# One written-out order of stages for a fused expert and attention block, with the maxima rows on Sync's queue

## The reference

```
# block 0, per sequence
nx = layer_norm(x) * gamma + beta
w  = softmax((nx @ Wq) @ (ctx @ Wk).T / sqrt(128));  evidence = w @ (ctx @ Wv)
c  = concat(nx, evidence, cond)
p  = softmax(c @ router_W + router_b)                      # 3 experts
h  = silu(c @ e_w1 + e_b1);  routed = sum_e p_e * (h_e @ e_w2_e + e_b2_e)
x  = x + sigmoid(silu(c @ gate_w1 + b) @ gate_w2 + b) * (routed @ out_w + out_b)
# block 1
m  = silu(cond) @ ada_w + ada_b                            # 6 shifts, scales, gates
x  = x + gate_msa * (attention16(qkv(norm(x) * (1 + scale) + shift)) @ self_o + b)
x  = x + attention16(q = norm(x) @ q_w, k, v = ctx @ kv_w) @ cross_o + b
x  = x + gate_mlp * (gelu((norm(x) * (1 + scale) + shift) @ w1 + b) @ w2 + b)
```

## Time and profile before

| | us |
|---|---|
| median of 3 runs | 326.23 |
| lowest, highest | 324.36, 326.57 |
| the profiled execution, its own time | 325.7 |
| its span | 323.9 |
| mean TensorE clock granted in it | 0.91 |

### The profile page before, as it was taken

The page is one execution under the profiler, slowest core; times in us unless marked ns, Lnnn a source line. Parts: engine busy times, 40 slices in busy tenths (PEclk is TensorE's granted clock), DMA queues, the critical chain, the costliest instruction groups (busy, mean ns, idle before and its releaser), DMA issues.

```text
span 323.9 us, 4780 instructions
## 1 busy us (share of the span) xinstructions
PE 255.5 (79%) x1784; PEld 145.0 (45%) x1802; DVE 180.1 (56%) x390; ACT 147.5 (46%) x271; POOL 43.8 (14%) x54
## 2 busy tenths in 40 slices
PE   3779999799467889279989899887997766748676
PEld 2765657358012344134534444543643433436356
DVE  6643317658979758337889757983131533250331
ACT  1213241542005476236665577569386342724442
POOL 1200420806001072000100010020010012000120
PEclk9999999999758999969999999999899795776979
DMA  7999900037410015620030002000003000200000
GB/s 205 393 131 173 169 2 0 0 98 177 134 55 5 3 51 148 133 63 2 2 92 9 6 3 87 14 5 0 18 17 84 2 3 2 78 20 21 0 0 32
DMA packets 15456, 19.71 MB, mean 61 GB/s; under 512 B 3234, under 2 KB 13474, under 8 KB 14442
## 3 DMA queue, kind: packets, MB, share of 16 engines
q1 hardware_dynamic: 15014, 19.22, 23.8%
q10 hardware_dynamic: 420, 0.20, 0.2%
HBM read 16.19 MB, written 3.03 MB: 59 GB/s over the span
## 4 chain that ended last, share of the span: by engine, by line
PE 54%; DVE 25%; ACT 7%; DMA 7%; issue 5%; SPq 1%; POOL 0%; ACTq 0%; DVEq 0%; POOLq 0%
PE ps L1172 47%; DVE neg_max L1050 7%; DMA Qs<-max_rows 4%; DVE normed L863 4%; DVE neg_max L1059 3%; ACT region L766 3%; PE ps L1430 2%; PE ps L1200 2%; DVE routed L1007 1%; DVE stats L847 1%; DMA Qs<-q_scr 1%; DMA x_sb<-in_x 1%; ACT max_rows L752 1%; PE ps L1375 1%; DVE mean_var L850 1%
## 5 line engine op out<-in xcount | busy, mean ns | idle before, releaser
L766 ACT ACTIVATE region<-ps 128x512 f32<-128x512 f32 (+1 forms) x160 | 86.7, 595 | 51.7 <-PE ps L1172 51.2
L1050 DVE TENSOR_REDUCE neg_max<-ps 128x2 f32<-128x1024 f32 x64 | 77.4, 1222 | 27.1 <-PE ps L1172 26.1
L1172 PE MATMUL ps<-Qs,k_room 128*128 128x256 bf16 x256 | 42.3, 283 | 10.8 <-DMA Qs<-max_rows 7.2
L1172 PE MATMUL ps<-k_room,Qs 128*128 128x512 bf16 x111 | 38.7, 426 | 7.5 <-DVE neg_max L1050 4.9
L1172 PE MATMUL ps<-region,V 128*32 128x256 f32 x512 | 41.3, 401 | 0.8 <-DMA Qs<-q_scr 0.5
L582 POOL TENSOR_TENSOR rstd<-var_eps,minus_half 128x2 f32<-128x2 f32 (+1 forms) x12 | 9.7, 811 | 218.0 <-DVE var_eps L852 218.0
L1172 PEld LDWEIGHTS ps<-Qs,k_room 128*128 128x128 bf16 x256 | 22.3, 100 | 30.4 <-ACT region L766 15.9
L1172 PEld LDWEIGHTS ps<-region,V 128*32 128x32 f32 x512 | 10.6, 109 | 22.7 <-issue 20.2
L1059 DVE TENSOR_REDUCE neg_max<-ps 128x8 f32<-128x616 f32 x16 | 12.0, 792 | 13.4 <-PE ps L1172 13.3
L1172 PEld LDWEIGHTS ps<-k_room,Qs 128*128 128x128 bf16 x128 | 11.7, 102 | 17.0 <-DVE neg_max L1050 13.1
L752 ACT ACTIVATE max_rows<-ps 24x256 bf16<-24x256 bf16 (+1 forms) x12 | 4.5, 374 | 31.1 <-PE ps L1375 31.1
(11 more groups left out here) (159 smaller groups left out, 344.7 us busy)
## 6 DMA issues: line engine op xcount, KB each, us to landing
Qs<-q_scr SPq DMA_DIRECT2D x24, 192.0 KB
k_room<-k_scr SPq DMA_DIRECT2D x4, 576.0 KB
...
q_scr<-q_parts SPq DMA_DIRECT2D x8, 192.0 KB, 2.0
...
w_attn<-in_w_attn SPq DMA_DIRECT2D x1, 896.0 KB, 10.5
...
```

The lines of the kernel that those rows point to most:

```text
L766: nc.scalar.activation(probs[0:rows_, s % UNITS, j0:j0 + CT // 2, :], ps[0:rows_, EXP0 + e % 2, :].rearrange("p (j n) -> p j n", n=TU), AC ...
L1050: nc.vector.tensor_reduce(neg_max[:, b, t, h:h + MH], ps[:, bank:bank + MH, :], axis=AX, op=ALU.max, negate=True).then_inc(max_read, 1)
L1172: return nc.tensor.matmul(out, lhsT, rhs, start=start, stop=stop)
```

## The change

`plan()` goes, and a text `ORDER` takes its place, word by word a stage. The table has more kinds of stage than before, as steps that hung on another stage now have a place of their own: `rows` (the DMA of maxima rows, issued by Sync and no longer by ScalarE), `send_keys`, `send_queries`, `load_keys`, `load_queries`, `load_cross`, `expert_bias`, `fold`, `add_bias`, `context_parts` and `weights:3`.

- Group self.0.0 is split, transposed and sent in two halves of four heads; exps of its first halves come first for all four key tiles.
- The products for the context leave `weights:2` for `weights:3`, behind queries:0, in banks MAX0 and MAX0 + 1; ScalarE copies them out and GpSimd splits the keys. `weights:2` moves ahead of hidden:0.4.
- route_norm:1 and expert_bias:1 come after the queries of sequence 1.
- Sequence 2's norm, keys, queries and values are placed singly among maxima and exps.
- `add_bias` waits for the normalisation behind its residual (`normed_ready`).
- `load_exp:1` is gone; mlp_down:0, project:self.3 and others stand elsewhere.

```diff
+ORDER = """
+scores:0 bias:0 scores_norm:0 scores_T:0 scores:1 evidence:0 bias:1 route:0 scores_norm:1 route_norm:0 hidden:0.0
+scores_T:1 hidden:0.1 hidden:0.2 hidden:0.3 weights:0 weights:1 weights:2 fold:0 expert_bias:0 hidden:0.4 hidden:0.5
+expert:0.0 hidden:0.6 evidence:1 gate:0 expert:0.1 expert:0.2 fold:1 route:1 expert:0.3 gated:0 stats:1.0 hidden:1.0
+hidden:1.1 apply:1.0 hidden:1.2 hidden:1.3 norm_T:1.0 add_bias:self.1 keys:0 queries:0 add_bias:self.0 weights:3
+send_keys:0 send_queries:0 load_keys:0.0 route_norm:1 load_queries:0 load_keys:0.1 load_queries:1 hidden:1.4
+hidden:1.5 values:0 hidden:1.6 expert_bias:1 gate:1 expert:1.0 expert:1.1 expert:1.2 context_parts:0 expert:1.3
+gated:1 max:0 max:1 max:2 max:3 max_split:self.0.0.0 max:4 max_T:self.0.0.0 max:5 max:6 max:7 rows:self.0.0.0 max:8
+max_split:self.0.0.1 max:9 max:10 max_T:self.0.0.1 load_exp:0 max:11 stats:1.1 rows:self.0.0.1 max:12 apply:1.1
+max:13 exp:self.0.0.0.0 exp:self.0.0.1.0 max:14 add_bias:self.2 max:15 max_split:self.0.1 norm_T:1.1 max:16
+exp:self.0.0.2.0 weigh:self.0.0.0.0 max_T:self.0.1 max:17 exp:self.0.0.3.0 weigh:self.0.0.1.0 rows:self.0.1 keys:1
+exp:self.0.0.0.1 max:18 weigh:self.0.0.2.0 max:19 weigh:self.0.0.3.0 queries:1 add_bias:self.3 weigh:self.0.0.0.1
+max:20 send_keys:1 exp:self.0.0.1.1 send_queries:1 exp:self.0.0.2.1 load_keys:1.0 load_queries:2 exp:self.0.0.3.1
+load_keys:1.1 exp:self.0.1.0.0 max:21 weigh:self.0.0.1.1 exp:self.0.1.0.1 max:22 exp:self.0.1.1.0 weigh:self.0.0.2.1
+max:23 load_queries:3 weigh:self.0.0.3.1 max_split:self.1.0 max_T:self.1.0 keep:self.0.0 weigh:self.0.1.0.0
+rows:self.1.0 max:24 max:25 exp:self.0.1.1.1 weigh:self.0.1.0.1 max:26 exp:self.0.1.2.0 exp:self.0.1.2.1
+weigh:self.0.1.1.0 values:1 weigh:self.0.1.1.1 exp:self.0.1.3.0 values_T:self.0.0 max:27 weigh:self.0.1.2.0
+exp:self.0.1.3.1 weigh:self.0.1.2.1 max:28 exp:self.1.0.0.0 max:29 weigh:self.0.1.3.0 exp:self.1.0.0.1 max:30 max:31
+exp:self.1.0.1.0 weigh:self.0.1.3.1 max_split:self.1.1 keep:self.0.1 exp:self.1.0.1.1 weigh:self.1.0.0.0
+max_T:self.1.1 exp:self.1.0.2.0 max:32 values_T:self.0.1 weigh:self.1.0.0.1 exp:self.1.0.2.1 max:33 heads_T:self.0
+weigh:self.1.0.1.0 max:34 exp:self.1.0.3.0 rows:self.1.1 weigh:self.1.0.1.1 project:self.0 stats:2.0
+exp:self.1.0.3.1 max:35 apply:2.0 max:36 weigh:self.1.0.2.0 exp:self.1.1.0.0 weigh:self.1.0.2.1 exp:self.1.1.0.1
+norm_T:2.0 max:37 add_bias:cross.0 weigh:self.1.0.3.0 query:0 max:38 exp:self.1.1.1.0 exp:self.1.1.1.1 max:39
+load_cross:0 weigh:self.1.0.3.1 keep:self.1.0 max_split:self.2.0 exp:self.1.1.2.0 max:40 max_T:self.2.0
+rows:self.2.0 max:41 weigh:self.1.1.0.0 max:42 weigh:self.1.1.0.1 exp:self.1.1.2.1 max:43 weigh:self.1.1.1.0
+exp:self.1.1.3.0 weigh:self.1.1.1.1 values_T:self.1.0 exp:self.1.1.3.1 max:44 weigh:self.1.1.2.0 exp:self.2.0.0.0
+cross_max:0.0 cross_max:0.1 cross_max:0.2 exp:self.2.0.0.1 max:45 cross_max:0.3 max_split:cross.0.0 exp:self.2.0.1.0
+weigh:self.1.1.2.1 weigh:self.1.1.3.0 max:46 max:47 exp:self.2.0.1.1 max_T:cross.0.0 max_split:self.2.1
...
+weigh:self.2.1.2.0 exp:self.3.0.1.0 max:60 weigh:self.2.1.2.1 apply:3.0 max:61 exp:self.3.0.1.1 norm_T:3.0
+exp:self.3.0.2.0 max:62 max:63 max_split:self.3.1 weigh:self.2.1.3.0 add_bias:mlp.0 weigh:self.2.1.3.1 mlp_up:0.0
+keep:self.2.1 mlp_up:0.1 max_T:self.3.1 weigh:self.3.0.0.0 exp:self.3.0.2.1 values_T:self.2.1 weigh:self.3.0.0.1
+rows:self.3.1 weigh:self.3.0.1.0 heads_T:self.2 exp:self.3.0.3.0 project:self.2 exp:self.3.0.3.1 exp:cross.1.0.0.0
+weigh:self.3.0.1.1 weigh:self.3.0.2.0 stats:2.2 apply:2.2 add_bias:cross.2 exp:cross.1.0.0.1 weigh:self.3.0.2.1
+norm_T:2.2 exp:cross.1.1.0.0 weigh:self.3.0.3.0 query:2 load_cross:2 exp:cross.1.1.0.1 weigh:self.3.0.3.1
+keep:self.3.0 exp:self.3.1.0.0 exp:self.3.1.0.1 weigh:cross.1.0.0.0 values_T:self.3.0 weigh:cross.1.0.0.1 mlp_down:0
+keep:cross.1.0 exp:self.3.1.1.0 weigh:cross.1.1.0.0 values_T:cross.1.0 exp:self.3.1.1.1 weigh:cross.1.1.0.1
+keep:cross.1.1 exp:self.3.1.2.0 weigh:self.3.1.0.0 values_T:cross.1.1 cross_max:2.0 weigh:self.3.1.0.1 cross_max:2.1
+exp:self.3.1.2.1 cross_max:2.2 cross_max:2.3 exp:self.3.1.3.0 heads_T:cross.1 weigh:self.3.1.1.0 exp:self.3.1.3.1
+max_split:cross.2.0 max_T:cross.2.0 project:cross.1 rows:cross.2.0 weigh:self.3.1.1.1 weigh:self.3.1.2.0 stats:3.1
+weigh:self.3.1.2.1 weigh:self.3.1.3.0 weigh:self.3.1.3.1 keep:self.3.1 values_T:self.3.1 apply:3.1 heads_T:self.3
+exp:cross.2.0.0.0 project:self.3 add_bias:mlp.1 stats:2.3 exp:cross.2.0.0.1 norm_T:3.1 weigh:cross.2.0.0.0 apply:2.3
+add_bias:cross.3 norm_T:2.3 weigh:cross.2.0.0.1 keep:cross.2.0 query:3 load_cross:3 values_T:cross.2.0
+exp:cross.2.1.0.0 weigh:cross.2.1.0.0 exp:cross.2.1.0.1 weigh:cross.2.1.0.1 keep:cross.2.1 mlp_up:1.0 mlp_up:1.1
+cross_max:3.0 cross_max:3.1 cross_max:3.2 cross_max:3.3 max_split:cross.3.0 values_T:cross.2.1 max_T:cross.3.0
+rows:cross.3.0 mlp_down:1 heads_T:cross.2 exp:cross.3.0.0.0 project:cross.2 exp:cross.3.0.0.1 weigh:cross.3.0.0.0
+stats:3.2 weigh:cross.3.0.0.1 exp:cross.3.1.0.0 keep:cross.3.0 exp:cross.3.1.0.1 values_T:cross.3.0
+weigh:cross.3.1.0.0 weigh:cross.3.1.0.1 keep:cross.3.1 apply:3.2 norm_T:3.2 values_T:cross.3.1 heads_T:cross.3
+project:cross.3 add_bias:mlp.2 mlp_up:2.0 stats:3.3 mlp_up:2.1 apply:3.3 norm_T:3.3 add_bias:mlp.3 mlp_up:3.0
+mlp_up:3.1 mlp_down:2 mlp_down:3
+"""
...
-        DELAY = dict(values_T=1, heads_T=2, project=3, stats=3, apply=5, norm_T=6, query=7, cross_max=13, rows=4,
-                     mlp_up=7, mlp_down=10)
-        NEXT = (0, 2, 3, 5, 7, 8)
...
+        CONTEXT_BANK = (MAX0, MAX0 + 1)
...
+            def load_cross(u):
+
+                sp.wait_ge(exp_raw, group_scored(("self", u, NG - 1)))
                 sp.wait_ge(q_out, 16 * Q_WRITES[("query", u)])
                 q_rows(u, NU + u)
...
+            def move_maxima(*group):
+
+                n = split_turn(*group)
+                u = group[1]
+                h0, nh = split_heads(*group)
+                sp.wait_ge(mT_ready, n + 1)
+                sp.dma_start(Qs[u][MROW:MROW + NPART, h0:h0 + nh, :],
+                             max_rows[0:NPART * nh, n % 2, :]).then_inc(m_in[n % 2], 16)
...
+            def split_context_keys():
+
+                pool.wait_ge(kc_ready, 1)
+                own(nc.gpsimd.tensor_copy(kc_parts[:, 0, :, :], kcf[:, :, :]))
+                own(nc.gpsimd.tensor_tensor(kc_rest[:, :, :], kcf[:, :, :], kc_parts[:, 0, :, :], ALU.subtract))
+                own(nc.gpsimd.tensor_copy(kc_parts[:, 1, :, :], kc_rest[:, :, :]))
+                tell(nc.gpsimd.tensor_tensor(kc_parts[:, 2, :, :], kc_rest[:, :, :], kc_parts[:, 1, :, :],
+                                             ALU.subtract), kc_split, 1)
...
                 if kind == "self":
-                    pool.wait_ge(x1_ready, b + 1)
+                    pool.wait_ge(normed_ready, NORM_TURN[(1, b)] + 1)
...
+            def keep_context():
+                act.wait_ge(ones_set, B)
+                act.wait_ge(kc_raw, 1)
+                nc.scalar.activation(kcf[:, :, 0:L], ps[:, CONTEXT_BANK[0], 0:B * L].rearrange("p (b n) -> p b n", b=B),
+                                     ACT.Identity, bias=col("kv_k")).then_inc(kc_ready, 1)
...
-                act.wait_ge(mT_ready, n + 1)
-                act.dma_start(Qs[u][MROW:MROW + NPART, h0:h0 + nh, :],
-                              max_rows[0:NPART * nh, n % 2, :]).then_inc(m_in[n % 2], 16)
...
+                if t == 0:
+                    pe.wait_ge(con_sb, made("e_out_w1"))
+                    pe.wait_ge(hid_ready, HC * b + HC - 1)
```

More of the change, by code:

```diff
@@ new lines @@
+apply:2.1 exp:cross.0.0.0.1 weigh:self.2.0.2.1 norm_T:2.1 max:51 exp:cross.0.1.0.0 weigh:self.2.0.3.0 query:1
+exp:cross.0.1.0.1 weigh:self.2.0.3.1 keep:self.2.0 exp:self.2.1.0.0 max:52 weigh:cross.0.0.0.0 max:53
+add_bias:cross.1 weigh:cross.0.0.0.1 exp:self.2.1.0.1 keep:cross.0.0 exp:self.2.1.1.0 load_cross:1 values_T:self.2.0
+max:54 weigh:cross.0.1.0.0 max:55 max_split:self.3.0 exp:self.2.1.1.1 values_T:cross.0.0 weigh:cross.0.1.0.1
+keep:cross.0.1 max:56 exp:self.2.1.2.0 weigh:self.2.1.0.0 max_T:self.3.0 cross_max:1.0 cross_max:1.1
@@ L451, in mixed_expert_attention_kernel @@
         MLP_TURN = {stage[1]: i for stage, i in turns("mlp_down").items()}
-        BIAS_TURN = {(stage[0], stage[1]): i for stage, i in turns("project", "mlp_down").items()}
+        BIAS_TURN = {stage[1]: i for stage, i in turns("add_bias").items()}
         def max_place(i):
@@ L1070, in split_maxima @@
                 part = [max_parts[:, :, i * nh:(i + 1) * nh] for i in range(NPART)]
[L1071 removed]
+                last = (("max", GROUP_MAX * NG * u + NTU * (h0 + nh) // MH - 1) if kind == "self" else
                         ("cross_max", (u, NH // CH - 1)))
@@ L1407, in weigh_values @@
                         pe.wait_ge(v_ready, b + 1)
+                    if kind == "cross" and g == 0:
+                        pe.wait_ge(vc_ready, B)
                     claim(PVB)
```

326 lines of the change are left out of this document (116 added, 210 removed).

## The result

| | us | ratio to the kernel before |
|---|---|---|
| before, median of 4 (lowest, highest) | 326.40 (324.36, 328.19) | |
| changed, median of 4 | 314.96 (313.91, 315.76) | 0.9649 [0.9585, 0.9713] |
| changed, its profiled execution | 315.2, span 313.4 | |

The change takes 3.5% off, and the profiled span is 10.5 us shorter, which is also what the prediction's terms add up to. Two of those terms missed by nearly 2 us each, in opposite directions. Two of the four runs of the old order in the new code (experiment 3), the profiled one among them, were in a slower state: its ratio goes by the other two, and only the transfer of its row is read from the profile.

A forecast was written before the change was run, and what follows sets the result against it. TensorE, busy 79% of the span, was taken as the bound, about 68 us idle. Terms -0.1 + 0.3 - 2.2 - 4.5 - 4.0 = -10.5 turn 325.7 into 315.2, median forecast 315.7 us, range 305 to 322.

The forecast's parts named there:

- Opening: Up to the first maximum: it moves from 84.84 to 83.7 us; this lead adds nothing to the sum by itself.
- The row: Maxima row of self.1.0, now behind Sync's loads: lands about 140.7, TensorE waits about 7 us; term -0.1 us.
- uneven order: Rival, chance 0.10: exps waiting for banks hold weighings behind them, fourteen pairs cost 9.8 us plus clock dips; 332.7 us.
- The pairs that I costed at nothing: Between max:12 and max:63, seven places of adjoining exps and seven of adjoining maxima: 0 to 9.8 us, taken as 0.
- the row comes first: Rival, chance 0.18: self.1.0's row is there before TensorE arrives, so the other 10 us go as well; 306 us.
- Sync's rows: Sync's other waits, load_cross:0 standing ahead of rows:self.2.0: costs 0 to +1.5 us, taken +0.3.
- Middle: Up to 223 us: transposes of maxima and splits stand better placed, adjoining pairs taken as 0; -2.2 us (-4.5 to +7.6).
- 223 to 262: That stretch of the span: -2.0 for mlp_up:0's wait, -2.5 for mlp_down:0's move, clock included; -4.5 us (-7 to -1).
- mlp_down:0's place: Moved behind query:2, it covers 2 us of that query's load: -2.5 us with its slow clock.
- End: Last part: project:self.3 earlier 2.2, two normalisations freed of port conflicts 2.2, table load 0.4 back; -4.0 us (-6 to -1).
- The two port conflicts: Late two-tile normalisations beside GpSimd's bias additions: 0.55 instead of 1.65 us each, 1.1 us back twice, 2.2 in all.
- Project:self.3's place: Near the end, no longer behind norm_T:3.1 and two exps: project:self.3 starts 2.2 us earlier.

The follow-up runs named there:

- experiment 3: The new kernel's code with its stages in the order of the kernel before, first group's maxima whole: ratio 1.0116 to the kernel before.
- experiment 6: Changed kernel with sequence 1's routing normalisation and expert bias put back ahead of its four normalisations: 318.74 us, ratio 0.9805 to the kernel before.
- experiment 2: Changed kernel with the transpose of self.1.0's maxima placed later: 316.56 us; with all maxima rows also on ScalarE's queue again: 314.4 us.
- experiment 1: Changed kernel with ScalarE again issuing every DMA of maxima rows from its own queue: 317.3 us, ratio 0.9797 to the kernel before.
- experiment 7: Changed kernel with project:self.3 and mlp_down:0 put back in their old places: 317.38 us, ratio 0.9757 to the kernel before.
- experiment 5: Changed kernel with GpSimd's output and mlp bias additions beside the normalisations again: 314.64 us, ratio 0.9672 to the kernel before.

## Why the prediction was right, and where not

The span fell by 10.5 us, as summed, and the median is 314.96 where 315.7 was forecast. The mechanism (the order gains, the row stays late) was right, and experiment 3 shows that without the order there is no gain. That the sum fits to a tenth is luck: the middle came out 1.5 us worse than its terms, 223 to 262 1.9 better, and the 7 us for which TensorE was to wait went elsewhere. By its steps:

*Opening.* Right on every row: the four normalisations took 1.11 us, the wait for the keys' copy 0.96, the experts began at 74.58 (74.9) and the first maximum at 83.27 (83.7), though other traces of the same opening have it between 82.2 and 83.7. Wrong was "none of this lead adds to the sum by itself, for the next DMA ends it". That DMA starts from queries:1, on the same stream, so it moves with the lead: experiment 6 puts 5.0 us on the first maximum and finds 4.6 at the end. Against the kernel before the lead is only 1.6 us at the first maximum and 1.8 at the query writes; my sum had the latter after all, as loads that start 2.5 us earlier, and was right there by its own step and not by the sentence. The place of the expert bias weighs more than I had it (2.7 us): now that no hidden layer stands between norm and keys:0, the conflict costs 2.1 us of wait and 2.9 of clock.

*The row.* Landing 141.16 (140.7), query writes 120.62 (120.0), term +0.35 (-0.1). The step that failed is "arrive near 133.5 and wait about **7 us**": it arrived at 140.7 and waited 0.5. Most of the 7 us went to the uneven order. The pairs that I costed at nothing cost 0.2 to 0.5 us each where exps of a self group adjoin (0.47, 0.20, 0.29 and 0.53 ahead of the row, and again 0.53 at 160.65 and 197.87), the transpose directly behind its split 1.58 and the weighing behind it 1.03, plus a clock at half. All this lay under the row's shadow, so it took nothing from the total; by experiment 2, taking part of it away buys nothing as long as the row is late. The same holds for the rival *the row comes first*, whose 306 us took all 10 us behind the row for gain: even with the row there at once, TensorE would have arrived at 140.7.

*Sync's rows.* I had +0.3; experiment 1 has a gain of 2.3. Two effects were missing: ScalarE is freed of 0.7 us for each of the 13 rows, and that outweighs the later landing of the one row that matters, since at that row TensorE came late in any case. With TensorE there early (experiment 2) ScalarE's queue does no worse. By the Trainium skill (DMA: Bandwidth & Descriptors, Queues, rings and completion order) a ring's descriptors are consumed in order while rings take turns; the table by queue agrees in its direction, 11.1 to 12.4 us from issue to landing on ScalarE's queue against 12.4 to 12.9 behind the loads on Sync's. That the other queue gains so little, turns or no turns, it doesn't explain.

*Middle.* -2.2 + 0.3 predicted for the transposes' places and Sync's other waits; from -0.35 behind the row to 0.1 at mlp_up:0 it is -0.4. And this holds two gains that the terms didn't have. The half clock behind the row, 1.8 us, is gone as TensorE no longer stood for 7 us there (granted 1.00 from 141.20 to 172.18), and Sync's rows give 1.0 from query:0 to query:1 alone. In that same stretch the kernel before takes 32.7 us, and the new order with ScalarE's rows (experiment 1) 34.5 with 1.0 us more work in it, so the order itself lost 0.8. The stops ahead of the values' transposes did go; stops of 0.5 before adjoining exps took part of that back, and what took the rest isn't shown.

*223 to 262.* -4.5 predicted; from 0.1 at mlp_up:0 to 6.5 at 262.62 it is -6.4. Mlp_up:0's 1.60 us wait is gone, and with it the clock of 0.66 from 224 to 229. The step that I had wrong is mlp_down:0's place, -2.5: by experiment 7 it is worth 0.5. The other waits of this stretch went with the rest of the order (before: 1.40 for an issue, 0.7 ahead of the heads' transpose, 0.7 for cross maxima, 0.5 for a query load), and I had counted none of them but a part of the issue. TensorE is granted 1.00 in all of 220.57 to 256.17, where it had 0.92. This error and that of the middle cancel.

*End.* -4.0 predicted, from 6.5 to 10.4: -3.9. Project:self.3 follows its heads by 0.97 us instead of 3.46:

```profile
257.60 0.41 PE L1425 MATMUL ps<-ident,heads 128*128 128x128 f32 x2 [0.77 <-DVE heads L1058]
...
258.57 0.68 PE L1141 MATMUL ps<-self_o,headsT 128*128 128x128 f32 x4
```

3.7 of the 3.9 are won by query:3. The two port conflicts are not worth 2.2 but 0.5 by the medians, and perhaps nothing (experiment 5; one of the two bias additions had gone from beside the norm with the order, and that half isn't measured by itself). Project:self.3's place is worth 2.9 to 3.3 (experiment 7) and not 2.2, a part of it the clock, 0.65 before and 0.90 now up to query:3. These errors largely cancel as well.

The rival *uneven order* had the right mechanism and the wrong place: of the 2.6 us that its adjoining exps cost in stops, 1.5 fell where a DMA was awaited anyway. (Adjoining maxima are eight by the table, not seven.) Its sign, waits for exp reads above 4.8, showed with 7.2; that for maxima reads didn't, with 4.4. The sign listed as wrong, a wait of VectorE for GpSimd's expert bias, did show (GpSimd worked at it from 71.00 to 76.98, and VectorE's first sum came at 77.07), but the sums' end hung on the last expert matmul at 80.1.
